# Routing inside the attention loop, and the row maximum turned as soon as it is there, in a gated attention and expert layer

## The reference, cut to what matters

```python
x = x + tanh(g_xattn[0]) * xattn(layernorm(x), ctx, ctx, wq, wk, wv, wo_w, wo_b)   # rope, band, softmax, 16 heads
x = x + tanh(g_ffn[0]) * ffn(layernorm(x), w_router, w_fc, w_gate, w_proj)

def ffn(x, ...):                       # E = 16 experts, K = 2, cap = 16 places per expert and sequence
    probs = softmax(x @ w_router)
    top_k_probs, ei = top_k(probs, K)
    pos = place of each token among those that chose the same expert, first choices before second ones
    buf[ei, pos] = x                   # tokens past cap are dropped
    h = silu(buf @ w_gate) * (buf @ w_fc)
    o = h @ w_proj
    return sum_k top_k_probs[k] * o[ei[k], pos[k]]
```

## Time and profile before

| | us |
|---|---|
| median of 3 runs | 1761.66 |
| lowest, highest | 1759.19, 1764.53 |
| profiled execution, its device time | 1754.3 |
| span of the profiled execution | 1752.5 |
| PE busy | 1481.3 (85%) |
| DVE busy | 1408.6 (80%) |
| ACT busy | 1146.4 (65%) |
| POOL busy | 1086.1 (62%) |

### The profile page before, as it was taken

One profiled execution on the slowest core, in us unless ns is written; L12 is line 12 of the kernel. 1 busy time (PEld: TensorE's weight loads), 2 busy tenths in 40 slices (PEclk: granted clock), 3 DMA queues, 4 the chain that ended last, 5 costly groups with the idle time before them and its releaser, 6 DMA issues. The chain is left out here.

```text
span 1752.5 us, 50746 instructions
## 1 busy us (share of the span) xinstructions
PE 1481.3 (85%) x16844; PEld 1195.2 (68%) x16844; DVE 1408.6 (80%) x2993; ACT 1146.4 (65%) x2321; POOL 1086.1 (62%) x1490
## 2 busy tenths in 40 slices
PE   3899999999999999999999999982199888888881
PEld 3676667777776676777676677761088888888881
DVE  3788888888888888878888888867878999999984
ACT  3777777777777777777777777764065555555550
POOL 3555656565655656565565656534638887888876
PEclk9999999999999999999999999995589999999995
DMA  3122121212222121212212121430037888888887
GB/s 94 50 76 75 61 89 60 90 60 84 65 67 82 60 90 60 90 60 78 71 62 88 60 90 60 137 119 30 15 106 245 260 261 258 261 273 263 264 261 223
DMA packets 156096, 210.21 MB, mean 120 GB/s; under 512 B 18688, under 2 KB 104832, under 8 KB 156032
## 3 DMA queue, kind: packets, MB, share of 16 engines
q1 hardware_dynamic: 125312, 142.36, 25.9%
q0 software_dynamic: 12288, 33.57, 6.7%
q10 hardware_dynamic: 18432, 33.56, 5.3%
HBM read 125.54 MB, written 83.89 MB: 119 GB/s over the span
## 5 line engine op out<-in xcount | busy, mean ns | idle before, releaser
L506 DVE TRANSPOSE_TENSOR_REDUCE part_max<-ST 128x16 f32<-128x512 f32 x512 | 321.3, 685 | 136.6 <-PE ST L685 136.6
L360 ACT ACTIVATE probs_t<-ST 128x512 f32<-128x512 f32 x512 | 264.4, 604 | 27.6 <-PE ST L700 27.4
L712 PE MATMUL PO<-probs_t,v_aug 128*32 128x128 f32 x4096 | 193.6, 284 | 67.9 <-ACT probs_t L360 55.4
L299 POOL TENSOR_TENSOR k_rot<-k_cos,k_sin 128x256 f32<-128x256 f32 x64 | 47.1, 736 | 268.5 <-DVE k_sin L544 268.5
L712 PEld LDWEIGHTS PO<-probs_t,v_aug 128*32 128x32 f32 x4096 | 88.9, 109 | 161.1 <-ACT probs_t L360 154.0
L1191 ACT ACTIVATE x_hi<-scaled 128x256 fp32r<-128x256 f32 x128 | 53.5, 418 | 214.8 <-DMA scaled<-xn_d 168.5
L401 ACT ACTIVATE at_hi<-F 128x512 fp32r<-128x512 f32 x64 | 38.2, 597 | 187.8 <-PE F L730 187.8
L1260 PE MATMUL GU<-we_hi,s_hi 128*128 128x256 f32 x512 | 155.4, 304 | 0.2 <-DVE s_lo L1250 0.2
L1154 POOL DMA_INDIRECT second<-eo_d,collect_row x128 | 123.0, 961 | 42.2 <-issue 28.6
L1163 POOL TENSOR_TENSOR x_lo<-scaled,x_hi 128x256 fp32r<-128x256 f32 x128 | 118.4, 925 | 49.3 <-ACT x_hi L1191 47.3
L1154 POOL DMA_INDIRECT first<-eo_d,collect_row x128 | 124.4, 972 | 37.3 <-issue 20.6
(11 more groups left out here) (158 smaller groups left out, 5610.7 us busy)
## 6 DMA issues: line engine op xcount, KB each, us to landing
eo_d<-eo ACTq DMA_DIRECT2D x128, 256.0 KB
x_in_sb<-x SPq DMA_DIRECT2D x64, 256.0 KB, 2.8
c_in_sb<-ctx_t SPq DMA_DIRECT2D x64, 256.0 KB, 2.9
xr_sb<-x SPq DMA_DIRECT2D x64, 256.0 KB, 4.0
x_d<-x SPq DMA_DIRECT2D x64, 256.0 KB, 4.0
xn_d<-xn SPq DMA_DIRECT2D x64, 256.0 KB, 4.2
scaled<-xn_d SPq DMA_DIRECT2D x128, 128.0 KB, 4.0
scaled<-x_d SPq DMA_DIRECT2D x128, 128.0 KB
```

The source lines that it names most:

```text
L360: act.activation(probs_t[:, b, i].rearrange("p j q -> p (j q)"), ST[i][:], ACT.Exp) \
L506: dve.tensor_reduce(part_max[:, i, 0], ST[i][:].rearrange("p (c l) -> p c l", l=32), AX_X, ALU.max, apply_transpose=True).then_inc(M["part ...
L712: last = pe.matmul(PO[32 * j:32 * j + 32, i * SEQ:(i + 1) * SEQ], v_aug[:, n.par, b, head], probs_t[:, b, i, j], start=True, stop=True)
```

## The change

It has three parts, in one edit.

1. **Routing in the attention loop.** `routing_block` is gone. Its work is done for four sequences at a time (a quad, tiles of 64 elements per partition, 128 where both choices are in one) in further lags of the attention step, from 3 to 9, each in every second step. Steps run on to 72, and 12 of them are unrolled at the start in place of 2. The weights of the experts are loaded in steps 4 to 8 and split at the end of the attention loop, the lo parts on DVE.
2. **The turned maximum.** PE `turn_max` comes after the first three matmuls of the query projection (b = 0) and ahead of both halves of the output projection (b = 1); `attention_t` goes behind `subtract_max`; on DVE att goes behind shift, and the second half of the input statistics behind the second shift; on ACT at_hi goes between the exponentials and ct_hi behind them; two values units stand ahead of the transposes of xn2 where there was one less.
3. **Experts.** POOL only gathers; x_lo is made on DVE. ACT computes Silu, so one of the two DVE instructions of the gate goes. Loads have rings of 4 in place of 3 and are asked for one unit earlier against their use, the output is built in the tile of x_d, and SP issues its loads ahead of the store.

The ranges of the steps in `run`, the same on every engine:

```diff
     def run(eng, step):
-        for c in range(-4, 2):
+        for c in range(-4, 12):
             step(Pair(0, c))
-        with eng.Fori(1, PAIRS // 2 - 2) as i:
+        with eng.Fori(6, PAIRS // 2 - 2) as i:
             step(Pair(i, 0))
             step(Pair(i, 1))
-        for c in range(PAIRS - 4, PAIRS + 2):
+        for c in range(PAIRS - 4, PAIRS + 9):
             step(Pair(0, c))
```

GpSimd, called in each step between the residual and `rotate`:

```diff
+        def route(s):
+            if quad(s, 4):
+                less_peak(quad(s, 4))
+            if quad(s, 5):
+                code_of(quad(s, 5), 0)
+            if quad(s, 7):
+                code_of(quad(s, 7), 1)
+            if quad(s, 9):
+                place_of(quad(s, 9))
```

ScalarE, the middle of a step; `exp_logits` is the exponential of 64 elements per partition:

```diff
+            if quad(s, 4):
+                exp_logits(quad(s, 4))
+            if s.beyond == -1:
+                weight_heads(0, 3)
+            if s.real:
+                exp_unit(s, 0, 0)
+                exp_unit(s, 0, 1)
             if (s - 1).real:
                 attention_head(s - 1)
             if s.real:
-                for i in range(4):
-                    exp_unit(s, 0, i)
+                exp_unit(s, 0, 2)
+                exp_unit(s, 0, 3)
                 copy_out_t(s, 0)
```

VectorE; the first group stands between q_sin and the partial maxima of b = 1, the second between att and k_cos:

```diff
+            if quad(s, 3):
+                find_peak(quad(s, 3))
+            if quad(s, 4):
+                find_first(quad(s, 4))
+            if quad(s, 5):
+                expert_of(quad(s, 5), 0)
+            if quad(s, 6):
+                find_second(quad(s, 6))
+            if quad(s, 7):
+                expert_of(quad(s, 7), 1)
+            if quad(s, 9):
+                rank_of(quad(s, 9))
...
+            if quad(s, 5):
+                compare(quad(s, 5), 0)
+            if quad(s, 6):
+                drop_first(quad(s, 6))
+            if quad(s, 7):
+                compare(quad(s, 7), 1)
+            if quad(s, 8):
+                mark_both(quad(s, 8))
```

The experts, their lags and the instructions on which x_lo and the gate change:

```diff
-    LOAD, PICK, DISPATCH, GATE, HIDDEN, OUTPUT, FETCH, COLLECT = -13, -11, -9, 0, 2, 3, 12, 14
+    LOAD, HEAD, PICK, DISPATCH, GATE, HIDDEN, OUTPUT, FETCH, COLLECT = -14, -11, -10, -9, 0, 2, 3, 13, 15
...
-                pool.tensor_tensor(x_lo[:, n.slot(2)], x_in_sb[:, n.turn(3)], x_hi[:, n.slot(2)].bitcast(F32),
-                                   ALU.subtract).then_inc(M["x_lo_done"], 1)
...
+                dve.tensor_tensor(x_lo[:, n.slot(2)], x_in_sb[:, n.turn(4)], x_hi[:, n.turn(4)].bitcast(F32),
+                                  ALU.subtract).then_inc(M["x_lo_done"], 1)
...
-                dve.scalar_tensor_tensor(out=th[:, n.slot(2)], in0=th[:, n.slot(2)], scalar=1.0, in1=gu[:, :, 0],
-                                         op0=ALU.add, op1=ALU.mult).then_inc(M["gated_done"], 1)
```

567 lines of the change are left out of this document (294 added, 273 removed).

## The result

In the comparison the changed kernel takes 1774.77 us (median of 4 runs, 1772.12 to 1778.81) where the kernel before takes 1760.43 (1759.05 to 1764.53): a ratio of 1.0077, with a 95% interval of 1.0059 to 1.0094. It is slower by 14 us, or 0.8%, where I had forecast 1701 and faster.

The account below looks back on a forecast made before the run. Bounds: chains of waits in attention and experts (x_d loads), no engine full; routing almost DVE alone. From 1754.3 us, -46 - 37 + 2.5 + 18 + 2 = -60.5 gives 1693.8; the execution lies 7.4 below the median, so 1701 (1662 to 1740).

Parts of the forecast that it names:

- The experts' term, -37: Experts: cutting the loop of x_d loads brings a unit from 3.43 to 3.10 us; -37 us, bounds 0 and -54.
- the attention's term, +18: Attention loop: added routing work, less 0.2 from the turn, costs 0.37 us a step over 48 steps; +18, 0 to +38.
- experts stay at 3.43 us: Rival, experts: loaded queues keep x_d transfers long, so units stay at 3.43 us; 37 us more, 1738; chance 0.17.
- experts at PE's floor: Rival: experts reach PE's 2.96 us a unit and the attention is unchanged; 1666 us, chance 0.04.
- The contention of x_lo and L1244: Experts: x_lo on POOL and L1244 on DVE slowed each other, 0.72 to 1.00 and 0.48 to 0.60 us.
- Routing block, -46: Between attention and experts: 56.3 us removed, 6.3 for the last quad, 0.5 barrier, 3 weights' split added; -46, -51 to -36.
- The turned maximum, b = 0: gain nothing: Attention, b = 0: subtraction 0.23 us earlier, but at_hi between the exponentials keeps ACT's string as long; no gain.
- b = 1: gain 0.2: Attention, b = 1: the turn ahead of the output projection gains 0.2 us a step, bounds 0 and 0.5.
- The contention rule in the attention, +0.2 a step: Attention: new DVE comparisons beside POOL's rotation would add about 0.2 us a step, +10 us by the skill's rule.
- Setup +2: Setup: four more tables loaded ahead of the inputs, at 0.47 us an issue, cost 2 us.
- Tail +2.5: End of the experts: FETCH and COLLECT lag one unit more, two gathers at the end; +2.5 us, 0 to 3.
- The slower rival: Rival, attention: six routing instructions at 0.53 us each make DVE the bound; +84 in place of +18, 1767 us, chance 0.06.

Follow-up runs that it names:

- e4: The changed kernel with the load of x_d left out from the fifth unit on: 1765.83 us, 3.48 us a unit.
- h1: The changed kernel, unaltered, on another chip than the comparison's: 1688.43 us, ratio 0.9585 to the kernel before.
- h2: The changed kernel with the b = 0 part of the turned maximum undone, on the same chip as h1: 1671.73 us.
- k2: The changed kernel, unaltered, on a further chip: 1687.46 us, ratio 0.9598 to the kernel before.
- k3: The changed kernel with the b = 0 part of the turned maximum undone, on the same chip as k2: 1670.35 us.
- e8: The kernel before with Silu in place of Tanh and one DVE instruction of the gate less: 1746.86 us, 3.30 us a unit.
- g3: The changed kernel with the b = 0 part undone and the expert block of before, but with Silu: 1720.68 us, ratio 0.9775.
- e7: The kernel before with the b = 0 part without its early turn, and x_lo on DVE in the experts: 1896.54 us.

## Why the prediction was wrong, by its own steps

Two steps failed. The experts' term, -37, was +20 in the comparison, since it put ACT's wait for TensorE's signals at nothing; why these signals are late stays open. And the attention's term, +18, missed what the b = 0 part of the turned maximum costs, which shows on every chip.

- **Experts, -37: the term that decided.** On the chip of the comparison it is +20 (19.5, and 0.5 for the start). What failed is the sentence that nothing in the earlier trace rows speaks of a ceiling below 3.08 us: ACT's starts came 82 us late in 95 units. I took a rate from one window of 10 us and a floor from the repeat of the earlier trace rows, and no row of the kernel before could have shown that its signals to ACT come late at a higher rate. The rival "experts stay at 3.43 us" names the nearest outcome, but for another reason: it blames the transfers, and e4 took a seventh of them away for nothing.
- **The same term on the other chips** is -64 (-64.6 and +0.5), beyond my lower bound of -54. The mechanism was right: the chain of x_d loads of the earlier trace rows is gone from the chain of waits, DVE's unit fell under 3 us, PE became the bound. The floor was mis-sized. The earlier trace rows are DVE's, and so is their wait of 0.36; on PE the next unit's GU products start 2.85 us later there (1295.85 and 1298.70), and 2.85 is also the distance of most units in h1. And 3.08 came from 78 matmul records in a trace that lacks some: 2731 in 394.3 us, where 24 a unit at 3.39 us make 2790. (The 3.36 us a unit of the prediction divides by 128; there are 127 distances, and it is 3.39.) The rival "experts at PE's floor" is what happened there.
- **The contention of x_lo and L1244** went as said: x_lo takes 418 ns on DVE, and the second of the collection 478 where the earlier trace rows has a median of 604.
- **Routing block, -46.** Measured -47.5 from the logits to the first load, where the terms without the split make -49.5: the last quad's chain took 8.8 us, not 6.8. The last steps of the attention, where I had 3 for the split of the weights, are 8.1 longer. I asked whether the split fits DVE's and ACT's holes, and not which instructions stand behind it on DVE nor whom it holds up on POOL.
- **The turned maximum, b = 0: gain nothing.** Wrong, +0.19 to 0.26 us a step, and 15 to 17 us up to pair 63 between two runs on the same chip (part_max of pair 63 less that of pair 0: 1169.4 in h1 and 1152.0 in h2, 1167.4 in k2 and 1152.3 in k3). The failed sentence is that ACT's string gets as long as it was, and the gain is nothing: by the timelines the string is as long, but it began before the subtraction was there and now can't. The turn by itself gains 0.12.
- **b = 1: gain 0.2.** Measured 0.06 to 0.13, at the low end of its bounds.
- **Routing in the loop, +18.** Without the b = 0 part it is +17 to +22 (1148.9 to 1153.8, less 1131.7 before), or 0.37 to 0.43 a step in place of 0.37. Right in size by luck: I had put 0.40 on the six instructions ahead of part_max of b = 1, which cost nothing (slack left: 0.80 us; 0.13 us apart, not 0.30). As far as the waits show it, the cost is in the marks ahead of k_cos, through at_lo and PSUM bank F2, and in the rank matmuls.
- **The contention rule in the attention, +0.2 a step.** The trace shows nothing of that size: POOL's rotation takes 727 to 741 ns in the changed kernel's loop and took 729 to 736 before.
- **Setup +2:** measured -0.8. **Tail +2.5:** measured +2.4 and +3.6.
- **The slower rival**, DVE as the bound of the attention (1767), comes near the time and is wrong in its mechanism: DVE still waits in every step.

On the two other chips the changed kernel took 1688 and 1687 us, near my 1701 by two errors that cancel: up to the first load of the experts 24 us worse than forecast (-2.4 in place of -26), the experts 27 better. The rest, some 9 us, is that the profile of before lies 7.4 us under its median and h1's 1.8 above. On the chip of the comparison only the first error is left, and the experts are 57 us worse than forecast.

k1 beats both kernels on the one chip where it was tried, 1666.81 us against 1687.46 (k2) and 1758.53: the change with the transposes ahead of the subtraction, att ahead of shift and at_hi ahead of the exponentials, as before.

## What to carry to other kernels

An instruction that fills a hole of its engine costs little; moved between two instructions of the critical string it can cost more than the wait that the move removes (here at_hi is 0.60 us long, and the string ended 0.30 later though it could begin 0.20 earlier). Look for that before counting what the move frees, and look as well at which PSUM bank a delayed reader holds. When several edits to a suspected stage give all the same time, stop editing the stage and run one program unaltered beside a known one on another chip, and come back to the first chip as well, which I did not.

## What the runs showed of the hardware

- The same program took 3.54 us a unit in the experts on one chip and 2.88 on two others, while its attention agreed to 0.01 us a step and the kernel before agreed within 0.3% on all. TensorE's signals reached ScalarE up to 2 us after their matmuls on the one. A schedule with room for it (e8, g3) took 3.30 and 3.29 us a unit on either kind. I had no such case in any range.
- A hole of some 1 us in PE, in two microseconds in which it was busy for 0.51 and 0.55, was followed by a granted clock of 0.80 and three times 0.50 in windows of 1 us, and a step 1.45 us longer (e7); a hole in the step before, busy for 0.71 and 0.34, was not.
- POOL's instructions on 128x2 elements go from 0.22 to 0.97 and 1.05 us beside DVE instructions of 1.15 us with two operands in SBUF.
- In the experts 315 GB/s went on for 310 us at a DMA share of 0.96, with PE busy for 306.7 of 310 us.
